# Scores and cosines of four graph layers as three products of rounded halves, in new engine sequences

## What is computed

```python
x = _layernorm(x + attention_0(x, adj))   # 4 heads of 64
x = _layernorm(x + gnn_1(x, adj))         # 4 heads of 256, tanh scores, gate
x = _layernorm(x + semantic_2(x))         # 8 heads of 32
x = _layernorm(x + attention_3(x, adj))   # 4 heads of 64
```

```python
sim = einsum('bhid,bhjd->bhij', q, k) * scale          # layers 0 and 3
attn = softmax(where(adj, sim, -max)); out = attn @ v

n = sem / max(norm(sem), 1e-8)                         # layer 2, sem = heads of m = x @ map_w.T + map_b
cos_adj = einsum('bhsd,bhtd->bhst', n, n) > 0.1
scores = einsum('bhsd,bhtd->bhst', q, k) / sqrt(32)    # q, k from m
adj = cos_adj * softmax(scores); Ax = adj @ sem_h
```

## Time and profile before

| | |
|---|---|
| median of 3 runs | 2700.77 us (2700.07 to 2704.37) |
| profiled execution | 2706.63 us |
| its span, first to last instruction | 2704.8 us |
| mean granted TensorE clock | 0.98 of full speed |
| PE busy | 2621.3 us (97%), 21649 matmul passes |
| weight loads (PEld) | 2314.8 us (86%) |
| DVE busy | 1958.7 us (72%) |
| ACT busy | 1399.0 us (52%) |
| POOL busy | 911.7 us (34%) |
| HBM read, written | 20.73 MB, 8.39 MB |

### The profile page before, as it was taken

One profiled execution on the slowest core, in us unless ns is written; L12 is line 12 of the kernel. 1 busy time (PEld: TensorE's weight loads), 2 busy tenths in 40 slices (PEclk: granted clock), 3 DMA queues, 4 the chain that ended last, 5 costly groups with the idle time before them and its releaser, 6 DMA issues.

```text
span 2704.8 us, 62514 instructions
## 1 busy us (share of the span) xinstructions
PE 2621.3 (97%) x21649; PEld 2314.8 (86%) x21649; DVE 1958.7 (72%) x6630; ACT 1399.0 (52%) x3893; POOL 911.7 (34%) x979
## 2 busy tenths in 40 slices
PE   8789999999999999999999999999999999999985
PEld 7778888888888988888898888888888889888873
DVE  2367777777777777777777777777777777777764
ACT  1345556455555555555555554555555565555442
POOL 1233333423333433323343333343332334333330
PEclk8899999999999999999999999999999999999996
DMA  4000000000000000000000000000000000000000
GB/s 132 1 7 10 11 2 10 10 10 10 9 1 10 10 10 10 9 10 1 10 10 10 10 9 1 10 10 10 10 10 9 1 10 10 10 10 9 5 2 8
DMA packets 44481, 29.77 MB, mean 11 GB/s; under 512 B 21264, under 2 KB 44048, under 8 KB 44432
## 3 DMA queue, kind: packets, MB, share of 16 engines
q1 hardware_dynamic: 44432, 29.13, 3.7%
HBM read 20.73 MB, written 8.39 MB: 11 GB/s over the span
## 4 chain that ended last, share of the span: by engine, by line
PE 93%; DVE 4%; issue 1%; ACT 0%; POOL 0%; DMA 0%; DVEq 0%; SPq 0%; POOLq 0%; ACTq 0%
PE bank L247 20%; PE bank L249 17%; PE bank L248 17%; PE bank L246 9%; PE bank L304 5%; PE bank L313 4%; PE bank L1151 4%; PE bank L236 4%; PE bank L1142 3%; PE bank L324 3%; PE bank L1133 3%; PE bank L1161 2%; DVE arena L420 2%; PE bank L723 1%; PE bank L982 1%
## 5 line engine op out<-in xcount | busy, mean ns | idle before, releaser
L178 POOL TENSOR_SCALAR l_ve<-l_mv 128x2 f32<-128x2 f32 x128 | 29.3, 229 | 1015.9 <-DVE l_mv L163 1015.8
L247 PE MATMUL bank<-arena_r 128*128 128x256 f32 x1024 | 303.6, 297 | 2.9 <-POOL arena_r L1556 1.8
L1296 ACT ACTIVATE b<-b,s_sh 128x256 f32<-128x256 f32 x512 | 254.0, 500 | 86.9 <-DVE s_sh L420 85.2
L248 PE MATMUL bank<-arena_r 128*128 128x256 f32 x1024 | 288.8, 282 | 0.0
L249 PE MATMUL bank<-arena_r 128*128 128x256 f32 x1024 | 288.5, 282 | 0.0
L1556 POOL TENSOR_TENSOR arena_r<-a,arena_r 128x512 fp32r<-128x512 f32 x128 | 165.6, 1294 | 344.4 <-ACT arena_r L1235 344.3
L247 PEld LDWEIGHTS bank<-arena_r 128*128 128x128 f32 x1024 | 194.4, 190 | 37.0 <-issue 33.6
L1457 DVE SCALAR_TENSOR_TENSOR b<-bank,b 128x256 f32<-128x256 f32 x512 | 186.0, 419 | 52.3 <-PE bank L1142 42.6
L1551 POOL TENSOR_TENSOR arena_r<-a,arena_r 128x512 fp32r<-128x512 f32 x128 | 164.2, 1283 | 163.7 <-ACT arena_r L1241 163.7
L248 PEld LDWEIGHTS bank<-arena_r 128*128 128x128 f32 x1024 | 195.1, 190 | 0.0
L249 PEld LDWEIGHTS bank<-arena_r 128*128 128x128 f32 x1024 | 194.9, 190 | 0.0
(11 more groups left out here) (273 smaller groups left out, 8783.9 us busy)
## 6 DMA issues: line engine op xcount, KB each, us to landing
x_in<-in_x SPq DMA_DIRECT2D x32, 256.0 KB, 2.8
out<-x SPq DMA_DIRECT2D x32, 256.0 KB, 2.1
adj_a<-in_adj SPq DMA_DIRECT2D x32, 64.0 KB, 2.5
adj_b<-in_adj SPq DMA_DIRECT2D x32, 64.0 KB, 1.9
a<-in_L_gnn_W SPq DMA_DIRECT2D x4, 256.0 KB, 3.6
b<-in_L_gnn_A_w SPq DMA_DIRECT2D x1, 1024.0 KB, 7.3
arena<-in_L_gnn_attn SPq DMA_DIRECT2D x4, 256.0 KB, 7.0
g_b_wh<-in_L_gnn_bW SPq DMA_DIRECT2D x1, 512.0 KB, 8.7
```

The lines of the kernel that those rows point to most:

```text
L247: pe.matmul(out, w[0], x[0], start=first, stop=False)
L248: pe.matmul(out, w[0], x[1], start=False, stop=False)
L1296: last = act.activation(S.e[:, n, it, :], S.e[:, n, it, :], ACT.Exp, bias=S.sh[:, it, h:h + 1], scale=-1.0, accum_out=S.sums[:, it, h:h + 1])
```

## The change

1. `scores`, `b_scores` and `b_cos` become three products each, in the same row strips: all strips with hi·hi, then hi·lo, then lo·hi, accumulated. `qt`, `kt`, `ut` become pairs of rounded halves. PE issues 12 instructions for a 64-row stage where it had 4 products (8 passes), 24 for a 32-row stage where it had 8 (16 passes).
2. ACT's copies write the high halves. New DVE stages `d_q`, `d_k`, `a_q`, `a_k`, `b_q`, `b_k`, `b_unit_t` write the low halves. They lie in places that are free then: `b32r` 0 and 1 (layer 2's input halves, so `b_q` and `b_k` wait on DVE for all four products that read those), arena places 9, 20 and 21 (so `b_unit_t` waits for layer 1's head products, and layer 1's last head waits for the cosines).
3. All four lists are new. They begin at other stages, and in between entries have moved.
4. One more turn is written out before the loop (`LAG + 2`).
5. Two pairs of semaphores of each norm become one of two counts each. ACT's `b_x_t` waits for layer 3's scores of the graph before.

```diff
-                last = pe.matmul(B[2 * pair + half][:, it * NODES:(it + 1) * NODES],
-                                 L.qt[rows, pair, it * P:(it + 1) * P], L.kt[rows, pair, :],
-                                 start=True, stop=True)
+            for n, (a, b) in enumerate(L.products):
+                for half in range(2):
+                    rows = slice(DHA * half, DHA * half + DHA)
+                    last = pe.matmul(B[2 * pair + half][:, it * NODES:(it + 1) * NODES],
+                                     L.qt[a][rows, pair, it * P:(it + 1) * P], L.kt[b][rows, pair, :],
+                                     start=(n == 0), stop=(n == len(L.products) - 1))
...
-        act.activation(L.qt[:, :, :], view(B[1]), ACT.Copy).then_inc(L.q_sb.sem, 1)
+        act.activation(L.qt[0], view(B[1]), ACT.Copy).then_inc((L.q_hi if L.fine else L.q_sb).sem, 1)
...
+    def q(g):
+        dve.wait_ge(L.q_hi.sem, L.q_hi.at(g))
+        dve_lower(dve, B[1], L.qt).then_inc(L.q_sb.sem, 1)
+
+    def k(g):
+        dve.wait_ge(L.k_hi.sem, L.k_hi.at(g))
+        dve_lower(dve, B[2], L.kt).then_inc(L.k_sb.sem, 1)
...
+        A.qt, A.kt = (a32r(14), a32r(9)), (a32r(15), a32r(20))
+        A.products = (0, 0), (0, 1), (1, 0)
...
+        D.qt, D.kt = (b32s(1), b32r(0)), (b32s(2), b32r(1))
+        D.products = (0, 0), (0, 1), (1, 0)
...
-        S.qt, S.kt, S.ut = b32(1), b32(2), b32(3)
+        S.qt, S.kt, S.ut = (b32s(1), b32r(0)), (b32s(2), b32r(1)), (b32s(3), a32r(21))
+        PRODUCTS = (0, 0), (0, 1), (1, 0)
...
-            for t in range(LAG + 1):
+            for t in range(LAG + 2):
                 body(t)
-            with eng.Fori(LAG + 1, GRAPHS) as t:
+            with eng.Fori(LAG + 2, GRAPHS) as t:
                 body(t)
...
                 for it in range(T):
-                    for n in range(QUAD):
-                        rows = slice(DHS * n, DHS * n + DHS)
-                        last = pe.matmul(BB[n][:, it * NODES:(it + 1) * NODES], S.qt[rows, q, it * P:(it + 1) * P],
-                                         S.kt[rows, q, :], start=True, stop=True)
+                    for k, (a, b) in enumerate(PRODUCTS):
+                        for n in range(QUAD):
+                            rows = slice(DHS * n, DHS * n + DHS)
+                            last = pe.matmul(BB[n][:, it * NODES:(it + 1) * NODES], S.qt[a][rows, q, it * P:(it + 1) * P],
+                                             S.kt[b][rows, q, :], start=(k == 0), stop=(k == len(PRODUCTS) - 1))
...
+                elif stage == "b_q":
+                    dve.wait_ge(S.m_psum.sem, S.m_psum.at(g))
+                    dve.wait_ge(S.k_psum.sem, S.k_psum.at(g))
+                    dve.wait_ge(S.sem_psum.sem, S.sem_psum.at(g))
+                    dve.wait_ge(S.q_hi.sem, S.q_hi.at(g))
+                    biased_lower(S.qt, BB[2], S.b_q).then_inc(S.q_sb.sem, 1)
...
+                elif stage == "b_unit_t":
+                    dve.wait_ge(G.ha_psum.sem, G.ha_psum.all(g))
+                    dve.wait_ge(S.unit_hi.sem, S.unit_hi.at(g))
+                    dve_lower(dve, BB[1], S.ut).then_inc(S.unit_sb.sem, 1)
```

Of the table, two lines of POOL's list, before and now:

```diff
-        ("g_wh_0", 1), ("g_a_0", 1), ("g_wh_1", 1), ("a_mask", 0), ("g_a_1", 1), ("g_wh_2", 1), ("d_mask", 2),
+        ("d_mask", 2), ("a_mask", 1), ("a_bias", 1), ("g_rstd", 2), ("a_rstd", 1), ("b_mask", 2), ("b_inorm", 2),
```

More of the change, by code:

```diff
@@ L138, in norm_signals @@
     N.sum = Signal(ctx, nc, f"{name}_sum")
[L139 to L142 removed]
+    N.stats_var = Signal(ctx, nc, f"{name}_stats_var", 2)
+    N.eps_rstd = Signal(ctx, nc, f"{name}_eps_rstd", 2)
     N.out = Signal(ctx, nc, f"{name}_out")
@@ L158, in dve_norm_stats @@
         last = dve.bn_stats(N.st[:, it, :], N.r[:, it, :])
-    last.then_inc(N.stats.sem, 1)
-    dve.wait_ge(N.stats.sem, N.stats.at(g))
+    last.then_inc(N.stats_var.sem, 1)
+    dve.wait_ge(N.stats_var.sem, N.stats_var.at(g, 1))
     apart(dve)
@@ L163, in dve_norm_stats @@
         last = dve.bn_aggr(N.mv[:, it, :], N.st[:, it, :])
-    last.then_inc(N.var.sem, 1)
+    last.then_inc(N.stats_var.sem, 1)
 def dve_norm_out(dve, N, g):
-    dve.wait_ge(N.rstd.sem, N.rstd.at(g))
+    dve.wait_ge(N.eps_rstd.sem, N.eps_rstd.at(g, 2))
     for it in range(T):
@@ L196, in attention_layer @@
     L.v_psum = Signal(ctx, nc, f"{name}_v_psum")
+    if fine:
+        L.q_hi, L.k_hi = (Signal(ctx, nc, f"{name}_{n}_hi") for n in "qk")
     L.q_sb = Signal(ctx, nc, f"{name}_q_sb")
@@ L301, in scores @@
         for it in range(T):
-            for half in range(2):
-                rows = slice(DHA * half, DHA * half + DHA)
-                last = pe.matmul(B[2 * pair + half][:, it * NODES:(it + 1) * NODES],
-                                 L.qt[rows, pair, it * P:(it + 1) * P], L.kt[rows, pair, :],
-                                 start=True, stop=True)
+            for n, (a, b) in enumerate(L.products):
[4 more added lines that the diff above has]
+                                     start=(n == 0), stop=(n == len(L.products) - 1))
         last.then_inc(L.s_psum.sem, 1)
@@ L373, in k @@
         act.wait_ge(L.k_psum.sem, L.k_psum.at(g))
-        act.activation(L.kt[:, :, :], view(B[2]), ACT.Copy).then_inc(L.k_sb.sem, 1)
+        act.activation(L.kt[0], view(B[2]), ACT.Copy).then_inc((L.k_hi if L.fine else L.k_sb).sem, 1)
     def exps(g, h):
@@ L480, in slot @@
             x_t(g)
+        elif what == "q":
+            q(g)
+        elif what == "k":
+            k(g)
         elif what == "v":
@@ L1139, in b_cos @@
                 for it in range(T):
-                    for n in range(QUAD):
-                        rows = slice(DHS * n, DHS * n + DHS)
-                        last = pe.matmul(BB[n][:, it * NODES:(it + 1) * NODES], S.ut[rows, q, it * P:(it + 1) * P],
-                                         S.ut[rows, q, :], start=True, stop=True)
+                    for k, (a, b) in enumerate(PRODUCTS):
+                        for n in range(QUAD):
+                            rows = slice(DHS * n, DHS * n + DHS)
+                            last = pe.matmul(BB[n][:, it * NODES:(it + 1) * NODES], S.ut[a][rows, q, it * P:(it + 1) * P],
+                                             S.ut[b][rows, q, :], start=(k == 0), stop=(k == len(PRODUCTS) - 1))
                 last.then_inc(S.cos_psum.sem, 1)
@@ L1317, in slot_b @@
                 if stage == "b_x_t":
+                    if later(g):
+                        act.wait_ge(D.s_psum.sem, D.s_psum.all(g - 1))
                     act.wait_ge(S.x_t_psum.sem, S.x_t_psum.at(g))
@@ L1376, in g_hp @@
             def g_hp(g, h):
+                if h == HG - 1 and later(g):
+                    dve.wait_ge(S.cos_psum.sem, S.cos_psum.all(g - 1))
                 dve.wait_ge(G.hp_hi.sem, G.hp_hi.at(g, h + 1))
@@ L1474, in spread_head, with biased_lower @@
                 return t.rearrange("p t (h a) -> p (t h) a", a=1).broadcast_to([P, T * HS, DHS])
+            def biased_lower(halves, bank, bias):
+                for jt in range(T):
+                    last = dve.scalar_tensor_tensor(halves[1][:, jt, :], bank[:, jt * NODES:(jt + 1) * NODES],
+                                                    bias[:, jt:jt + 1], halves[0][:, jt, :].bitcast(F32),
+                                                    ALU.add, ALU.subtract)
+                return last
             def slot_b(stage, g):
```

77 lines of the change are left out of this document (44 added, 33 removed), and 43 rows, old and new, of the table ORDER.

## The result

The changed kernel takes **2797.49 us** (2793.69 to 2800.67, 4 runs) against 2701.74 (2700.07 to 2704.37, 4 runs) for the kernel before: ratio **1.0353**, 95% interval 1.0335 to 1.0371. It is slower by 96 us. The forecast was 2768, the range 2668 to 2830. Each trace is of one execution: that of the changed kernel is of the one that took 2793.69.

What follows compares the result with a forecast made beforehand. PE was taken to bound the kernel nearly everywhere, DVE in the attentions. 32 x (0.3 + 1.8) + 2 = +69 us on 2706.6 gave 2775, less 5.9 for the median 2769, stated as 2768; range 2668 to 2830.

Steps and rivals of the forecast that it cites:

- The likeliest case: Attentions: added DVE work plus one meeting of POOL's masks with DVE, as summed; 2735 to 2795 us, chance 0.36.
- The products: PE's 32-row score and cosine stages: three rounded products take 0.95 us instead of 1.09, 0.14 less per stage.
- does not shorten: Attentions: PE's gain on the four stages there saves no time, since PE waits there anyway.
- The floor of 0.068 a pass: PE's score and cosine stages: rival that passes cannot be fed faster, 0.54 us more per stage, +87 us; chance 0.05.
- DVE's chain: Attentions: DVE's new order followed with old durations from D's first projection; A's values end at 23.55, 0.57 us later.
- The masks at the ports: Attentions: POOL's masks and bias additions block DVE's two normalisations of D at the SBUF ports, +1.8 us a turn.
- -0.35 a_out wait: A's output projection on PE: its wait of some 0.35 us for DVE's lower half of the values goes.
- the 0.3 of the sum: Whole turn: net of all terms except the meetings at the ports, +0.3 us a turn, +10 us in all.
- The moved masks on GpSimd: POOL's additive masks of A and D, moved from the graph layer into the attentions, delay DVE: +1.8 us a turn.
- One more costs nothing: Ahead of the loop: the extra written-out turn adds no time, since the 79.7 us came from a written-out turn.
- Ramp and tail: Start and end of the program: each exposed score stage has one more DVE hop (0.8), +2 us in all.

Runs made afterwards that it cites:

- the run with both moves: Changed kernel with POOL's two masks moved out of the attentions and its low half of the fourth W h behind that head's attention-matrix low half: 2717.87 us, ratio 1.0051.
- the first run: Changed kernel with only POOL's two masks moved out of the attentions, D's earlier and A's behind D's 1/std: 2742.64 us, ratio 1.0138.

## Why the prediction came out as it did

The likeliest case (slower, by work and meetings on DVE and POOL in the attentions) is what happened; the time is 29 us above the forecast, 2 above that case's own range. By its terms:

- **The products.** Forecast 0.14 a stage, measured 0.18 from one stage to the next; the turn loses 0.5 to 0.6 without those of the middle layer, 0.14 each. PE's gain in the attentions "does not shorten" them: right to 0.1 us a turn, by the run with the old products. The floor of 0.068 a pass is wrong: 24 passes in 0.91 us are 0.038 each. By the floor that the Trainium skill states (TensorE: Matmul & The Clock Gate, Back-to-back issue gap) for a TensorE without hardware decoding, 62 ns a matmul, the stage would by estimate have taken at least 1.49; the trace shows that this floor did not hold here.
- **DVE's chain** T by T: first mask 6.7, measured 6.61; copy of A's v done 12.97, measured 13.08; second normalisation done 14.2, measured 15.60; A's normalisations 20.85, measured 22.08; A's values 23.55, measured 24.86. Without the port wait (1.2 to 1.3) it fits to 0.15, and the run with both moves has A's values done at 23.58, against 23.55 forecast.
- **The masks at the ports**, 1.8 a turn: mechanism right, **mis-sized and misplaced**, 1.25. I let the first multiplication wait for the whole of D's mask (1.5); it lost 0.4, and the three behind it nothing. The second normalisation was given 0.4 and lost 1.27. PE pays it in full, as the first run shows.
- **"-0.35 a_out wait"** did not come: A's output projection still takes 1227.69 to 1229.49. The net of everything but the meetings is 0.8 a turn (the run with both moves), not the 0.3 of the sum. In the attentions it is the 0.6 that the sum has; outside them it is +0.2 instead of -0.3. This wait is one cause. Another may be the meeting of L1401 that stays in that run.
- **The step that failed** is "The moved masks on GpSimd" as a complete list of what moved on POOL. The new list also moves the low halves of W h: the second head's now stands right behind that of its attention matrix, the fourth head's ahead of it, and both meet L1401. The fourth head's costs 0.85 a turn, which the sum has at nothing. I had priced only instructions with one input in SBUF; in the kernel before this multiplication takes 690 ns in the mean.
- **The clock** was in no term: 11 turns of 30 at +1.6, **0.59 a turn**. It does not stand apart from the waits: of the two runs that each took away one meeting, the one without the masks' has no such turn, and the one without that of L1401 has 2 longer ones.
- **"One more costs nothing"** was the wrong question: it costs nothing, but without it the change would have taken 2854.
- **Ramp and tail** were put at +2 and gave -18: D's first projection starts at 202.7 (before 214.06), from the last but one of them to the last it is 63.8 (before 70.3). The earlier start comes with the new sequences: in every run with them it lies between 201 and 208, in those with the old ones between 214 and 216. The shorter last interval does not (64.5 to 70.3 with the old ones, 63.8 to 68.5 with the new); which entries matter was not tried.

The sum in hindsight: 1.25 + 0.85 + 0.59 + 0.8 = 3.49 us a turn, which is 83.22 - 79.73 (it has to close, since the 0.8 is what the other moves leave); by 30 turns 105, less 18: +87, as in the spans. The forecast had 2.1 x 32 + 2 = 69. Two of the four terms were missing, one was 0.55 too high and one 0.5 too low, and the 20 us by which ramp and tail were off took back nearly half of what was missing. That the forecast came nearer than its parts is luck; that it is slower, and by meetings with POOL while DVE is on the path, is not.

## What to carry to other kernels

A faster stage on the bounding engine is worth next to nothing in a stretch where another engine, which now also has to prepare its operands, is the one that ends last; put the finer products only where that engine has room. When lists of several engines are rewritten together, go through *every* pair of SBUF instructions on DVE and POOL that the new lists bring side by side, not only those that the change is about. If turns written out and turns in a loop differ in length, look at the instruction queues before you look for a wait.
